# A root-finding attention stage: lam minus score formed by TensorE for every pass

## The reference, cut to what matters

```python
s = einsum('bhnd,bhmd->bhnm', Q, K) * scale          # causal
lam = s_masked.max(-1) + 1.0
for _ in range(4):
    d = maximum(lam[..., None] - s, EPS)
    w = where(mask, 1 / d, 0.0)
    f = w.sum(-1) - 1.0
    fp = -where(mask, d ** -2, 0.0).sum(-1)
    lam = lam - f / fp
p = where(mask, 1 / maximum(lam[..., None] - s, EPS), 0.0)
p = p / p.sum(-1, keepdims=True)
out = einsum('bhnm,bhmd->bhnd', p, V)
```

## Time and profile before

| | us |
|---|---|
| median of two runs | 6142.75 (6131.52 to 6153.98) |
| span of the profiled execution | 6153.6 |
| last TensorE instruction of the first stage ends | 2688.7 |
| busy over the span: PE / DVE / ACT / POOL | 5086.1 / 4768.3 / 3546.7 / 2569.4 |

### The profile page before, as it was taken

How to read it: one execution, slowest core, us unless ns; L and a number is a source line. 1 busy time by engine, 2 the same in 40 slices (tenths; PEclk the granted TensorE clock), 3 DMA queues, 4 the chain that set the end, 5 groups by cost and what they waited for, 6 DMA issues and landing times. The chain is left out here.

```text
span 6153.6 us, 167056 instructions
## 1 busy us (share of the span) xinstructions
PE 5086.1 (83%) x61548; PEld 2941.8 (48%) x61548; DVE 4768.3 (77%) x11291; ACT 3546.7 (58%) x6859; POOL 2569.4 (42%) x1151
## 2 busy tenths in 40 slices
PE   6777767676767776769999998999899999989996
PEld 3444444444444444435555554555455545545553
DVE  5777777777777777848888887888788888878884
ACT  4777776777767776745545554455454545444552
POOL 1101011111101011136666676667666667666672
PEclk9999999999999999999999999999999999999997
DMA  0000000000000000024445444444444444444443
GB/s 11 3 3 6 1 8 1 6 3 6 3 6 3 6 0 6 1 67 103 103 109 122 108 101 105 109 115 106 108 105 103 116 114 104 100 106 115 110 108 84
DMA packets 231561, 383.60 MB, mean 62 GB/s; under 512 B 35712, under 2 KB 60928, under 8 KB 230656
## 3 DMA queue, kind: packets, MB, share of 16 engines
q1 hardware_dynamic: 226560, 370.71, 25.6%
q10 hardware_dynamic: 4224, 2.10, 0.1%
HBM read 51.81 MB, written 18.87 MB: 11 GB/s over the span
## 5 line engine op out<-in xcount | busy, mean ns | idle before, releaser
L386 ACT ACTIVATE R<-S,lam 128x128 f32<-128x128 f32 (+3 forms) x2560 | 1191.1, 551 | 200.6 <-DVE lam L528 158.3
L447 POOL TENSOR_TENSOR W<-R 128x1280 f32<-128x1280 f32 x128 | 309.9, 2441 | 2335.6 <-ACT R L386 2335.6
L212 PE MATMUL psS<-kT,qT 8*128 8x128 f32 (+3 forms) x1056 | 755.3, 816 | 311.5 <-DVE S L489 222.2
L517 DVE CUSTOM_DVE_ANT_0 R<-R 128x128 f32<-128x128 f32 (+3 forms) x2048 | 987.1, 536 | 14.1
L1300 POOL TENSOR_TENSOR m<-m 128x1024 f32<-128x1024 f32 x384 | 902.5, 2361 | 69.7 <-DVE m L1408 69.4
L506 DVE CUSTOM_DVE_ANT_0 R<-R 128x128 f32<-128x128 f32 (+3 forms) x1024 | 503.3, 523 | 495.5 <-ACT R L386 471.3
L917 PE MATMUL pb<-xs,wg 128*128 128x512 f32 x1536 | 763.4, 632 | 49.8 <-DMA xs<-hist 36.5
L238 PE MATMUL psO<-vals,WT 128*128 128x9 f32 x2640 | 587.0, 356 | 160.8 <-ACT WT L358 160.8
L238 PEld LDWEIGHTS psO<-vals,WT 128*128 128x128 f32 x2640 | 589.4, 331 | 209.5 <-ACT WT L358 209.5
L1431 DVE SCALAR_TENSOR_TENSOR nf<-rn,m 128x1024 f32<-128x1024 f32 x384 | 617.0, 1638 | 87.5 <-ACT rn L1162 74.7
L1153 ACT ACTIVATE lnn<-pb,cst 128x1024 f32<-128x1024 f32 x192 | 213.9, 1114 | 803.0 <-PE pb L924 803.0
(11 more groups left out here) (112 smaller groups left out, 8709.3 us busy)
## 6 DMA issues: line engine op xcount, KB each, us to landing
qkn<-nf SPq DMA_DIRECT2D x1536, 128.0 KB
vr<-v SPq DMA_DIRECT2D x96, 768.0 KB, 6.0
vr<-v SPq DMA_DIRECT2D x96, 192.0 KB, 5.6
xr<-hist SPq DMA_DIRECT2D x48, 256.0 KB, 2.9
hist<-xo SPq DMA_DIRECT2D x48, 256.0 KB, 4.1
wg<-wqkv SPq DMA_DIRECT2D x24, 384.0 KB, 3.6
xs<-hist SPq DMA_DIRECT2D x48, 128.0 KB
vr<-v SPq DMA_DIRECT2D x96, 64.0 KB, 6.2
```

The costliest lines, as they stand in the source:

```text
L212: pe.matmul(psS[:, u, 0:UNIT[u]], qT[32 * h:32 * h + DH1, j, u * P:(u + 1) * P], kT[32 * h:32 * h + DH1, j, 0:UNIT[u]], start=True, stop=True)
L386: nc.scalar.activation(R[:, h, c], S[:, par, h, c], ACT.Abs_reciprocal_sqrt, bias=lam[:, par, i:i + 1], scale=-1.0).then_inc(s_root, 1)
L517: nc.vector.tensor_tensor_reduce(out=R[:, h, c], in0=R[:, h, c], in1=R[:, h, c], scale=1.0, scalar=0.0, op0=ALU.mult, op1=ALU.add, accum_o ...
```

## The change

**Passes.** There is no `S` and no `R` any more. A ninth row joins each head's `qT` (lam, per query) and `kT` (the constant 1), and the keys are scaled by the negative of the score factor when they are moved out of PSUM. One matmul of nine rows then gives lam - s directly, and TensorE forms it anew for each of six passes of a quad: pass 0 with lam 0 for the maximum, four Newton passes, and the last one in transposed order (keys on partitions), which makes the later transposes unnecessary. Each pass of a head is four f32 matmuls (512, 384, 128 and 256 columns) into three PSUM banks and three bf16 mask matmuls (128, 256 and 128 columns):

```diff
+                for i, h in enumerate(heads):
+                    free(i)
+                    r = slice(32 * h, 32 * h + KROW)
+                    if p < LAST:
+                        for u in UORD:
+                            pe.matmul(psD[i][:, UOFF[u]:UOFF[u] + UNIT[u]], qT[r, j, u * P:(u + 1) * P], kT[r, j, 0:UNIT[u]],
+                                      start=(u != UORD[2]), stop=True, skip_group_check=True)
+                        spans = ((UOFF[3] + 3 * P, 1), (UOFF[2] + 2 * P, 2), (UOFF[1] + P, 1))
+                    else:
+                        for k in KORD:
+                            pe.matmul(psD[i][:, KOFF[k]:KOFF[k] + KLEN[k]], kT[r, j, k * P:(k + 1) * P], qT[r, j, k * P:SEQ],
+                                      start=(k != KORD[2]), stop=True, skip_group_check=True)
+                        spans = ((KOFF[0], 1), (KOFF[3], 2), (KOFF[2], 1))
+                    for c, n in spans:
+                        mm = pe.matmul(psD[i][:, c:c + n * P], identb[:, :],
+                                       cmaskb[:, int(p == LAST), 0:n, :].rearrange("p a n -> p (a n)"),
+                                       start=False, stop=True, skip_group_check=True)
+                    mm.then_inc(s_d, 1)
```

**ScalarE and VectorE.** A root and a square now take a whole head of 1280 columns from PSUM and SBUF, and VectorE gets both sums from bn_stats (one instruction per unit), followed by eight small instructions for a whole quad:

```diff
+                    nc.scalar.activation(dst, psD[i][:, 0:ROW], ACT.Abs_reciprocal_sqrt, bias=zero[:, 0:1])\
+                        .then_inc(s_rootf if p == LAST else s_root, 1)
...
+                    nc.scalar.activation(W[:, h, :], W[:, h, :], ACT.Square).then_inc(s_w, 1)
...
+                ins = nc.vector.bn_stats(out=stats[:, s % 2, i, :], in_=W[:, h, UOFF[u]:UOFF[u] + UNIT[u]])
...
-                                    nc.scalar.activation(R[:, h, c], S[:, par, h, c], ACT.Abs_reciprocal_sqrt,
-                                                         bias=lam[:, par, i:i + 1], scale=-1.0).then_inc(s_root, 1)
...
-                nc.vector.tensor_tensor(lam[:, par, c], lam[:, par, c], step[:, 1, c], ALU.add).then_inc(s_lam, 1)
```

**The way of lam.** The last of the small instructions transposes lam on VectorE, and SP sends it to row 9 of `qT` with four small transfers per pass:

```diff
+                for q in range(4):
+                    sp.dma_start(qT[DH1:P:32, j, :].rearrange("h (u q p) -> h u q p", u=NBLK, q=4)[:, :, q, :],
+                                 lamT[32 * q:32 * q + NU, j, :]).then_inc(lam_in[j], 16)
```

**The order.** A sequence is 24 slots, each one pass of one quad. A quad's passes lie four slots apart, so four quads (also of the next sequence) are under way at once:

```diff
+NSLOT = 24
+LAST = ITERS + 1
+SLOTS = {}
+for _j in range(NQ):
+    for _p in range(LAST + 1):
+        SLOTS[(5 * _j + 4 * _p) % NSLOT] = (_j, _p, (5 * _j + 4 * _p) // NSLOT)
```

**Output.** GpSimd squares the last root in place in `WF`, and `weigh` multiplies its ten blocks per head with the values as they stand. The transposes (L225) and ScalarE's copies of them (L358) are gone:

```diff
+                for u in range(NBLK):
+                    o = (u * QUAD + h) * VW
+                    for k in range(u + 1):
+                        c = KOFF[k] + (u - k) * P
+                        mm = pe.matmul(psO[:, o:o + VW], WF[:, h, c:c + P], vals[:, k, j * QUAD + h, :],
+                                       start=(k == 0), stop=(k == u))
```

More of the change, by code:

```diff
@@ L107, in stage1 @@
         zero = sb("zero", [P, 1])
-        psS = ps("psS", [P, NBLK, SEQ])
-        psT = ps("psT", [P, 2, SEQ])
+        psD = [ps(f"psD{i}", [P, BANKS1 * SEQ]) for i in range(2)]
         psO = ps("psO", [P, SEQ])
@@ L141, in stage1, with live, prev @@
         s_rs = [sem("s_rs_in"), sem("s_rs_out")]
-        M_PRO, M_B = 9, 13
-        E_PRO, E_B = 9, 12
+        held = {e: sem(f"held1_{e}") for e in ("pe", "act", "pool", "dve", "sp")}
+        M_PRO, M_B = 3, 13
+        E_PRO, E_B = 3, 12
         LN = 8
         block = ctx.enter_context(nc.Block())
+        def live(b, s):
+            return not isinstance(b, int) or 0 <= b - SLOTS[s][2] < BATCH
+        def prev(b, s):
+            while True:
+                b, s = (b, s - 1) if s else (b - 1, NSLOT - 1)
+                if isinstance(b, int) and b < 0:
+                    return None
+                if live(b, s):
+                    return b, s
@@ new lines, in rank, with fits, junk @@
+        def rank(b, s, passes, quad=None):
+            def fits(t):
+                return SLOTS[t][1] in passes and (quad is None or SLOTS[t][0] == quad)
+            if isinstance(b, int) and b == 0:
+                return sum(fits(t) for t in range(NSLOT) if t < s or not live(b, t))
+            return b * sum(fits(t) for t in range(NSLOT)) + sum(fits(t) for t in range(s) if live(b, t))
+        def junk(passes, quad=None):
+            return sum(SLOTS[t][1] in passes and (quad is None or SLOTS[t][0] == quad) for t in range(NSLOT) if SLOTS[t][2])
@@ L161, in store, with store_x1 @@
+            def store_x1(b):
                 sp.wait_ge(s_x1, b + 1)
+                sp.sem_inc(held["sp"], 1)
                 sp.dma_start(tokens(x1d, b - 1), x1[:, :, :]).then_inc(x1_out, 16)
[L163 to L167, removed]
-                first = isinstance(b, int) and b == 0
[L169 to L178, removed]
@@ L201, in turn_h @@
                 mm.then_inc(s_m, 1)
-            def project(which, j, n_ev):
-                m_free(n_ev)
-                pe.matmul(psM[:, :], wqk[:, which, j, :], hT[:, :], start=True, stop=True).then_inc(s_m, 1)
[L207 to L240, removed]
@@ L252, in turn_attn, with values @@
+            def values(n_ev):
+                m_free(n_ev)
+                for k in range(NBLK):
+                    mm = pe.matmul(psM[:, k * P:(k + 1) * P], hT[:, k * P:(k + 1) * P], wvo[:, 0, :], start=True, stop=True)
+                mm.then_inc(s_m, 1)
+            def turn_attn(b, n_ev):
+                pe.wait_ge(s_attn, rank(b, 12, FINAL) + 1)
+                pe.sem_inc(held["pe"], 1)
+                m_free(n_ev)
                 for k in range(NBLK):
@@ L267, in turn_out, with body @@
                 mm.then_inc(s_m, 1)
[L269 to L276, removed]
+            def body(b):
+                e = b * E_B + E_PRO
+                tail = isinstance(b, int) and b == BATCH
+                first = isinstance(b, int) and b == 0
+                for s in range(NSLOT):
+                    for pair in range(2):
+                        if live(b, s):
+                            differences(b, s, pair)
+                        for f in (1, 6, 11, 20):
+                            if s == f + 1 + pair and live(b, f):
+                                weigh(b, f, 2 * pair)
+                                weigh(b, f, 2 * pair + 1)
+                        if not tail:
+                            if (s, pair) == (2, 0):
+                                project(0, 1, e)
+                            if (s, pair) == (2, 1):
+                                project(1, 1, e + 1)
+                            if (s, pair) == (7, 0):
+                                project(0, 2, e + 2)
+                            if (s, pair) == (7, 1):
+                                project(1, 2, e + 3)
+                            if (s, pair) == (12, 0):
+                                project(0, 3, e + 4)
+                            if (s, pair) == (12, 1):
+                                project(1, 3, e + 5)
+                            if (s, pair) == (14, 0):
+                                values(e + 6)
+                        if (s, pair) == (15, 1):
+                            turn_attn(b, e + (0 if tail else 7))
+                        if (s, pair) == (16, 1):
+                            out_project(e + (1 if tail else 8))
+                        if (s, pair) == (20, 0):
+                            turn_out(b)
+                        if not tail:
+                            if (s, pair) == (21, 0):
+                                turn_h(e + 9, b * LN + 2 * LN)
+                            if (s, pair) == (22, 0):
+                                project(0, 0, e + 10)
+                            if (s, pair) == (22, 1):
+                                project(1, 0, e + 11)
@@ L549, in _ @@
+            hcount = fixed[:, 1:].rearrange("p (c t) -> p c t", t=2)
             nc.vector.memset(attn[:, :, :], 0.0)
-            dve.wait_ge(const_in, 64)
+            dve.wait_ge(cleared, 1)
+            dve.wait_ge(const_in, 96)
             nc.vector.tensor_copy(identb[:, :], ident[:, :]).then_inc(masks, 1)
-            nc.vector.tensor_copy(cmaskb[:, :], cmask[:, :]).then_inc(masks, 1)
+            for a in range(2):
+                ins = nc.vector.tensor_copy(cmaskb[:, :, a, :], cmask[:, :, :])
@@ L553, in _ @@
+            ins.then_inc(masks, 1)
             dve.wait_ge(masks, 2)
```

562 lines of the change are left out of this document (316 added, 246 removed).

## The result

The changed kernel takes 8129.49 us (median of 8128.6 and 8130.37) against 6142.75 us: a ratio of 1.322, with a 95% interval of 1.315 to 1.329. The forecast was 8170 us, in a range of 8000 to 8450.

A forecast was written before the change was run, and what follows sets the result against it. ScalarE and VectorE bound the first stage before; afterwards TensorE at 1.2 GHz would. 19 + 3917 + 569 + 191 + 20 = 4716 us against 2689 gave 8181, forecast as 8170 us, range 8000 to 8450.

The forecast's parts named there:

- The level of the clock: First stage: TensorE runs at 1.2 GHz, 1.027 us per 128x512 f32 record; the printed 1.00 means nothing was recorded.
- R1: Rival: full TensorE brings 2.4 GHz in the first stage, a head 2.55 us, kernel 5858 us; chance 0.06.
- The argument from the 31 us of scores: Before the change, 31 us of unbroken eight-row score matmuls brought no clock rise; nine rows were expected to do the same.
- A head at 5.10 us: One head of one pass on TensorE: 4.27 + 0.29 + 0.43 + 0.11 = 5.10 us, 768 heads 3917 us.
- half of the 0.22 us: A 128-column mask's 0.22 us to the next start, split into 0.11 for columns and 0.11 for the change of rows.
- 5.44: Head cost in us if the mask's whole 0.22 us goes by columns; the kernel would take 8430 us.
- all of the 0.40: Fixed parts of a head's price, 0.29 us for f32 matmuls and 0.11 for masks, all put on changing rows.
- The terms: First-stage sum on TensorE: start 19, heads 3917, output 569, projections and transposes 191, waits 20, together 4716 us.
- R2: Rival: each matmul of a head pays its own fixed part, 6.19 us a head, 9010 us; chance 0.04 including costs towards it.
- R3: Rival: two heads in different row groups overlap on TensorE, saving 1640 us, kernel 6530 us; chance 0.01.
- R4: Rival: clock rises for part of the first stage, around projections and output; at a third, 7400 us; chance 0.04.
- The other engines: ScalarE, VectorE, GpSimd and lam's transfers stay hidden behind TensorE's 20.4 us slot while TensorE is at the lower clock.

The follow-up runs named there:

- the one-mask kernel: Changed kernel (nine rows) with only the first of a head's three mask matmuls, for timing alone: 7910.1 us.
- the interleaved kernel: Changed kernel (nine rows) with the four difference matmuls of a pair's two heads issued in turn, then both heads' masks: 7024.98 us.

## Why the prediction was right, and where not

- **The level of the clock**, on which all hung, was read rightly. The page's 9s and the 1.00 stand in the changed kernel's first stage too, while its records last as at 1.2 GHz. In the traces of the kernels with 64 and 128 rows the row shows 0.50 and 0.91 in that stage, since there the clock moved. The clock records of the changed kernel's trace begin at 4694 us, in the second stage, so the 1.00 before it stands for no record at all. One comparison under R1 was made with the wrong length: eight records of 512 columns that follow each other take not 8.2 us at 1.2 GHz but about 7.2 (0.85 from start to start, and the end of the last). The 5.92 of the earlier trace rows is still shorter, and the reading stands.
- **The argument from the 31 us of scores** The earlier trace rows held for 4650 us of nine rows and for 32 rows. The Trainium skill (TensorE: Matmul & The Clock Gate, Part 1: The HAM clock gate) speaks of the engine's busy-ness; here 399.52 busy us of 400 stood at the lower level on 64 rows, and the same columns on 128 rows at the higher, so rule and measurement differ, and the measurement decides.
- **A head at 5.10 us** was exact, and the one-mask kernel confirms the mask's price by columns (4.78 without 384 of them). That half of the 0.22 us goes by columns was a guess, and a lucky one: 0.32 / 384 is 0.83 ns a column, 0.107 us for 128. The upper end, 5.44 for a mask that goes wholly by columns, is out. That all of the 0.40 is the change of rows was wrong; the head of 128 rows keeps 0.12 of it.
- **The terms.** Counted in the trace from each record's start to the next: start 21.3 (19 forecast), heads 3899 (3917), output 546, that is 0.213 us a record (569), projections and transposes behind the start 185 (191), TensorE's waits 20 (20). Together they are 4672 against 4716. The surplus of 44 us is the output by 23, the heads by 18 and the projections by 6. The heads come out lower because 128 of the 768 are followed by other work on all rows, not by nine rows, and take 4.96 us instead of 5.10. The record of the output is shorter here than the mean of the earlier trace rows; why stays open.
- **R1** was worth 5858 us in my sum. The engine was full, as R1 has it, and the clock did not rise. With the clock raised by rows the kernel came to 6095 at best, so its price was too low as well: the clock doesn't stay up through the output matmuls, and a head of 64 rows is 843.88 - 841.20 = 2.68 us at 2.4 GHz. That is 0.24 above the 2.44 of 128 rows, so the change of rows costs nearly what it does at 1.2 GHz (0.28), where the sum halved it.
- **R2** is out: four f32 matmuls with different weights follow each other in 2005.93 - 2001.37 = 4.56 us, 4.27 of it for the columns, which leaves 0.29 for all of them together.
- **R3** I gave 0.01 for the changed kernel, and for it that was right, but for a reason that I had only half. I leaned on four heads of scores that follow each other at 6.32 us. That row doesn't speak against overlap: a mask on all rows stands behind every unit there. The second reason, the mask between any two heads, is the one that the kernels without masks show. The Trainium skill (same page, Part 3: Packing small matmuls — row/col tiling) says that small matmuls on distinct row groups run concurrently, and the interleaved kernel agrees, 5.39 us for two heads.
- **R4**, a rise around the projections and the output, didn't come either: the stage has no clock record. The last output run, 80 records on all rows without a pause, takes 17.18 us at 1.2 GHz. Work on all rows is not enough if its matmuls have nine columns.
- **The other engines** were hidden as forecast, with TensorE waiting 22 us in the whole stage; lam's four transfers were waited for twice, 8.5 us.

## What to carry to other kernels

Before work is moved to TensorE, price its columns at the clock that it will have there: compare the duration of one form in two stages, since a granted clock of 1.00 can mean that nothing was recorded. A matmul of few rows costs the time of a full one and may keep the whole stage at half speed; zero-padding the operands to all rows took 1946 us off here, for three more copies of the keys per quad. Where padding is too dear, put independent small matmuls on different row groups and issue them in turn, and keep instructions that use all rows out from between them.

## What the runs showed of the hardware that I had not expected

- Heads of 64 rows kept the higher level, for 49 us twice, but every one of the four rises came behind 1.9 to 2.0 us of records on all 128 rows. Three of the falls came 2.2 to 2.7 us into the output records, with TensorE busy.
- Rows that work at the same time seem to count together: two heads on 64 rows each brought a rise 3.9 us after a wait of 7 us, with nothing on all rows between, and the clock rose 315 times in that stage. One head of 64 rows at a time never rose without records on all rows before it.
- Zeros count: in the kernel with 128 rows all but nine of a head's 128 rows of keys are zero, and the clock rose all the same.
- f32 matmuls of nine rows from different heads, in different row groups, overlap even when issued one head behind the other, 3.15 us for a head of 4.27 us of streaming, if nothing on all rows stands between.
- Output matmuls of nine columns on all rows, whose weight loads start every 0.213 us at 1.2 GHz, let the clock fall: behind 40 of them in the kernel with 128 rows, and still behind 20 when they were spread.
